# Sandwich block on one core: loading and splitting the weights in place, first token tile chunk by chunk, its gate and up products first

## The chip, the cores and the metric

The kernel runs on 1 core of one Trainium2 chip. The metric is the device time of one launch in microseconds (us). All arrays are float32. TensorE multiplies in a reduced format (fp32r), so the kernel splits each operand into a high part (rounded) and a low part (the rest), and three matmuls stand for one exact product: high by low, low by high, high by high.

## The reference, cut to what matters

```python
x = x + _layernorm(_L0_attn_ref(_layernorm(x), w_gate, w_up, w_down))
x = x + _layernorm(_L0_ffn_ref(_layernorm(x), W_gate, W_up, W_down))

def _L0_attn_ref(x, w_gate, w_up, w_down):
    s = jax.nn.silu(jnp.einsum('bsh,ih->bsi', x, w_gate))
    k = int(0.5 * I)
    _, idx = jax.lax.top_k(-jnp.abs(s), k)      # the k smallest |s| of each token
    s = s with those entries set to 0
    s = s * jnp.einsum('bsh,ih->bsi', x, w_up)
    return jnp.einsum('bsi,hi->bsh', s, w_down)
def _L0_ffn_ref(x, W_gate, W_up, W_down):
    return (silu(x @ W_gate.T) * (x @ W_up.T)) @ W_down.T
```

x has 4 x 512 = 2048 tokens of H = 512, and I = 1376. In the first layer half of the 1376 gate values of every token, the smallest in magnitude, are set to zero, so a threshold has to be found for each token.

## The kernel before, in words

The 2048 tokens are 16 tiles of 128 (j = 0 to 15). The second layer follows the first and is not touched by the change.

**A tile of layer 1.** x is normalised on VectorE (`x_stats`, GpSimd's power in `x_rstd`, `x_normalise`); for tiles 0 to 2 TensorE transposes it (`transpose_x`), for later tiles VectorE turns 32 x 32 blocks and a DMA moves them (`move_x`). ScalarE writes the high part (`split_x_hi`), VectorE the low part (`split_x_lo`). TensorE makes 3 gate products and 3 up products (n = 0 to 2, columns of 460, 460 and 456; `product(j, m, n)`, m = 0 gate, m = 1 up), each of 4 chunks of the contraction times 3 matmuls. In `product` a chunk is low weights, low x, high by high, and so on to the next chunk. ScalarE takes the silu of each gate product, VectorE the absolute values and their sum (`abs_values`).

**The search for the threshold.** It is a loop over three engines: ScalarE counts the values below the threshold (`count(j, n)`, n = 0 to 5), GpSimd moves the threshold (`newton(j, n)`, a `move` and a `thr` instruction), ScalarE counts again. Then VectorE reads the exact value off (`find_below`, `find_top`, `find_flag`), zeroes the small ones and multiplies (`select`), and turns blocks (`swap_h`). Four DMAs (`move_h`) bring it to transposed place, ScalarE and VectorE split it (`split_h_hi`, `split_h_lo`), and TensorE multiplies by w_down (`down(j)`, 33 matmuls). y is normalised (`y_stats`, `y_rstd`, `normalise_y`) and added to x. `times_up(j, n)` multiplies by the up product and frees its bank.

**The weights.** w_gate and w_up come in 12 pieces (w = 0 to 11: two chunks of the contraction by the columns of one n, 460 KB), w_down in 6 more (w = 12 to 17, 512 KB). SyncE loads each piece into one of 4 slots of a buffer `stage`; from the fifth on it waits until the slot's last piece has been split (L488). ScalarE copies stage to the high part (L905), VectorE subtracts it from stage and writes the low part (L1234).

**The order.** Every engine's instructions stand in an order written by hand; nothing is planned by costs. Before the change TensorE does gate 0.0, gate 0.1, the transposes of tile 1, gate 0.2, gate 1.0 to 1.2, then up 0.0, up 1.0, up 0.1, up 0.2, transposes of tile 2, up 1.1, up 1.2, then tiles 2 and 3 (from tile 2 on all gate, then all up), with `down(0)` behind gate 3.0 and `down(1)` behind up 3.2. From tile 4 on a loop is used; there `down(j-2)` stands behind up j.2 for j = 4, up j.1 for j = 5, and up j.0 from j = 6 on. VectorE's order begins at L1523, ScalarE's at L1057, SyncE's at L570, GpSimd's at L1806. `keep_busy` are transposes without a use that fill TensorE's first microseconds.

Of the kernel before, what the change touches and what calls it, by code (L numbers as in the profile page):

```python
# [16 lines left out]
def sandwich(nc, x, x_first, w_gate, w_up, w_down, W_gate, W_up, W_down, out):  # L17
# [47 lines left out]
    NSLOT = 4  # L65
# [11 lines left out]
    USEQ = [(0, 0), (1, 0), (0, 1), (0, 2), (1, 1), (1, 2)] + [(j, n) for j in range(2, TILES) for n in range(3)]  # L77
# [68 lines left out]
    with ctx:  # L146
# [22 lines left out]

        with nc.sbuf_tensor("stage", [P, NSLOT, 2, H], F32) as stage:  # L170
            pass
# [72 lines left out]

        prod_flat = prod[:, :, :].rearrange("p a b -> p (a b)")
        SW = KC * GW // 2
        stage_flat = stage[:, :, :, :].rearrange("p s c t -> p (s c t)")
# [101 lines left out]
        stage_in = [sem(f"stage_in{i}") for i in range(NSLOT)]  # L349
# [21 lines left out]
        x_moved = [sem(f"x_moved{i}") for i in range(2)]  # L371
        exact = sem("exact")
# [16 lines left out]
        ring = [("G", 0, 0), ("G", 0, 1), ("G", 0, 2), ("G", 1, 0), ("G", 1, 1), ("G", 1, 2)]  # L389
        ring += [("U", j, n) for j, n in USEQ[:6]]  # L390
        for j in range(2, TILES):
# [38 lines left out]
        def x_bank(a):  # L430

            return (tr_ps[1], tr_ps[2], tr_ps[1])[a]

# [8 lines left out]
        def _(sp):  # L442
# [41 lines left out]
            def load_w(w):  # L484
                m, n, c = PIECES[w]
                slot = w % NSLOT
                if w >= NSLOT:
                    sp.wait_ge(wlo_done, w - NSLOT + 1)  # L488
                if m < 2:
                    src = (w_gate, w_up)[m].rearrange("p (c i) -> p c i", c=KC)[:, c:c + 2, CO[n]:CO[n] + CW[n]]  # L490
                    sp.dma_start(stage[:, slot, :, 0:CW[n]], src).then_inc(stage_in[slot], 16)
                else:
                    src = w_down[n * P:(n + c) * P, :].rearrange("(c q) h -> q c h", q=P)
                    sp.dma_start(stage[:, slot, 0:c, :], src).then_inc(stage_in[slot], 16)
# [90 lines left out]
            for w in range(12, NP - 1):  # L585
# [4 lines left out]
            load_w(NP - 1)  # L590
# [101 lines left out]
        def _(pe):  # L692
# [23 lines left out]

            def product(j, m, n):
# [6 lines left out]
                for c in range(KC):  # L724
                    if j == 0 and c % 2 == 0:
                        pe.wait_ge(wlo_done, 6 * m + 2 * n + c // 2 + 1)
# [130 lines left out]
            product(1, 1, 1)  # L857
            product(1, 1, 2)
# [36 lines left out]
        def _(act):  # L895
            def split_weights_hi(w):
                m, n, c = PIECES[w]
                slot = w % NSLOT
                act.wait_ge(stage_in[slot], 16 * (w // NSLOT + 1))
                if m < 2:  # L900
                    src = stage[:, slot, :, 0:CW[n]]
                    dst = gu_hi[m][:, :].rearrange("p (c i) -> p c i", c=KC)[:, c:c + 2, CO[n]:CO[n] + CW[n]]
                else:
                    src, dst = stage[:, slot, 0:c, :], down_hi[:, n:n + c, :]
                nc.scalar.activation(dst, src, ACT.Copy).then_inc(whi_done, 1)  # L905
# [37 lines left out]
            def split_x_hi(a):  # L943
# [9 lines left out]
                nc.scalar.activation(hi, src, ACT.Copy).then_inc(xhi_done, 1)  # L953

# [103 lines left out]
            split_x_hi(0)  # L1058
            for w in range(1, 4):
                split_weights_hi(w)  # L1060
            silu(0, 0)
            split_weights_hi(4)
            split_weights_hi(5)
            silu(0, 1)
            split_x_hi(1)
            split_weights_hi(6)
            silu(0, 2)
            split_weights_hi(7)
            split_weights_hi(8)
# [12 lines left out]
            count(0, 4)
            split_x_hi(2)
            count(0, 5)
            split_weights_hi(13)
            guess(1)
            count(1, 0)
            split_weights_hi(14)
            count(1, 1)
            split_weights_hi(15)  # L1090
            count(1, 2)
            split_weights_hi(16)
            count(1, 3)
            split_x_hi(3)
            count(1, 4)
            silu(2, 0)
            split_h_hi(0)
# [5 lines left out]
            for n in range(4):  # L1103
                count(2, n)
            normalise_y(0)
            count(2, 4)
            split_h_hi(1)
            for j in range(3, TILES - 1):
# [8 lines left out]
                if j < TWO[0]:  # L1117
# [93 lines left out]
        def _(dve):  # L1211
# [11 lines left out]
            def split_weights_lo(w):  # L1223
                m, n, c = PIECES[w]
                slot = w % NSLOT
                dve.wait_ge(whi_done, w + 1)
                if m < 2:
                    src = stage[:, slot, :, 0:CW[n]]
                    hi, lo = (t[m][:, :].rearrange("p (c i) -> p c i", c=KC)[:, c:c + 2, CO[n]:CO[n] + CW[n]]
                              for t in (gu_hi, gu_lo))  # L1230
                else:
                    src = stage[:, slot, 0:c, :]
                    hi, lo = down_hi[:, n:n + c, :], down_lo[:, n:n + c, :]
                nc.vector.tensor_tensor(lo, src, hi.bitcast(F32), ALU.subtract).then_inc(wlo_done, 1)  # L1234
# [12 lines left out]
            def x_normalise(a):  # L1247
# [4 lines left out]
                if p >= FIRST:  # L1252
                    dve.wait_ge(xn_done, p + 1)
                    nc.vector.transpose(xin[:, p % 2, :], xin[:, p % 2, :]).then_inc(xswap_done, 1)

# [268 lines left out]
            x_normalise(0)  # L1524
            split_weights_lo(0)
            split_x_lo(0)
            for w in range(1, 4):
# [392 lines left out]
```

## Time and profile before

| | us |
|---|---|
| median of 3 runs | 725.38 (725.26 to 725.48) |
| the profiled execution | 725.1 |
| its span | 723.3 |
| TensorE busy in the span | 710.0 |
| VectorE busy | 569.3 |
| ScalarE busy | 380.0 |
| GpSimd busy | 246.5 |

The span runs from the first to the last instruction; 1.8 us of the profiled execution lie around it. The granted clock of TensorE was 0.998 of full speed over the span.

### The profile page before, as it was taken

What the parts mean: (1) busy time and instruction counts of PE and PEld (TensorE: products, weight loads), DVE (VectorE), ACT (ScalarE), POOL (GpSimd) and SP (SyncE); (2) the same over time, 40 slices, a digit from 0 to 9 for tenths busy, and PEclk for the clock granted to TensorE, in tenths of its full rate; (3) what the DMA queues carried; (4) which work ended last, traced back from release to release, by engine and by line L of the source; (5) the groups of instructions that cost most, each with busy time, mean ns of one, the idle gap of its engine ahead of it and who ended that gap; (6) DMA issues with size and microseconds to landing.
All of it is one profiled execution on the core that took longest, in us unless ns stands there. A gap on an engine that the chain in (4) does not pass through costs nothing.

```text
span 723.3 us, 9783 instructions
## 1 busy us (share of the span) xinstructions
PE 710.0 (98%) x3193; PEld 596.5 (82%) x3193; DVE 569.3 (79%) x980; ACT 380.0 (53%) x594; POOL 246.5 (34%) x372
## 2 busy tenths in 40 slices
PE   8999999999999999999999999999999999999996
PEld 7888788888888888888888888878877888877885
DVE  7789788889889888896889489987777898876342
ACT  5886577666666756667563234433344333323231
POOL 0422223332222332223241156613456665621001
PEclk9999999999999999999999999999999999999999
DMA  8641424333455344554322986345752533334441
GB/s 272 202 111 62 97 70 99 63 82 89 108 128 112 85 96 91 129 118 101 106 89 61 226 254 194 102 139 133 210 138 78 156 117 117 100 101 140 143 136 44
DMA packets 126214, 88.56 MB, mean 122 GB/s; under 512 B 66416, under 2 KB 106608, under 8 KB 126160
## 3 DMA queue, kind: packets, MB, share of 16 engines
q1 hardware_dynamic: 126160, 87.91, 45.0%
q8 instruction: 25, 0.41, 0.2%
q14 instruction: 29, 0.24, 0.1%
HBM read 49.87 MB, written 18.87 MB: 95 GB/s over the span
## 4 chain that ended last, share of the span: by engine, by line
PE 71%; DVE 8%; issue 7%; POOL 6%; ACT 5%; DMA 2%; SPq 0%; DVEq 0%; POOLq 0%; ACTq 0%
PE gu_ps L804 13%; PE y_ps L745 13%; PE gu_ps L731 11%; PE tr_ps L804 10%; PE tr_ps L731 8%; PE gu_ps L826 5%; PE tr_ps L826 4%; PE gu_ps L779 3%; PE tr_ps L779 3%; ACT junk L928 2%; POOL move L1769 1%; DMA stage<-in_L_attn_w_gate 1%; POOL yrstd L1753 1%; DVE below L1363 1%; POOL thr L1772 1%
## 5 line engine op out<-in xcount | busy, mean ns | idle before, releaser
L928 ACT ACTIVATE junk<-absv,thr 128x1383 bf16<-128x1383 f32 x96 | 139.1, 1449 | 42.9 <-POOL thr L1772 42.1
L745 PE MATMUL y_ps<-down_hi,hT 128*128 128x512 f32 x352 | 109.0, 391 | 0.0
L1769 POOL TENSOR_SCALAR move<-sgn 128x1 f32<-128x1 f32 x80 | 42.4, 530 | 107.6 <-ACT junk L928 107.5
L745 PEld LDWEIGHTS y_ps<-down_hi,hT 128*128 128x128 f32 x352 | 66.1, 188 | 14.4
L745 PE MATMUL y_ps<-down_lo,hT 128*128 128x512 f32 x176 | 69.3, 394 | 0.4 <-DVE hT L1273 0.4
L731 PE MATMUL gu_ps<-gate_hi,xT 128*128 128x460 f32 (+1 forms) x232 | 67.5, 372 | 0.0
L731 PE MATMUL gu_ps<-up_hi,xT 128*128 128x460 f32 (+1 forms) x232 | 67.2, 371 | 0.0
L1753 POOL TENSOR_TENSOR yrstd<-yvar,half 128x1 f32<-128x1 f32 x32 | 22.3, 696 | 91.8 <-DVE yvar L1282 91.7
L731 PEld LDWEIGHTS gu_ps<-gate_hi,xT 128*128 128x128 f32 x232 | 43.9, 189 | 4.9
L731 PEld LDWEIGHTS gu_ps<-up_hi,xT 128*128 128x128 f32 x232 | 43.6, 188 | 5.1
L1746 POOL TENSOR_TENSOR xrstd<-xvar,half 128x1 f32<-128x1 f32 x32 | 22.9, 715 | 68.6 <-DVE xvar L1245 68.5
L1804 POOL TENSOR_TENSOR prod<-prod,gate_lo_raw 128x512 f32<-128x512 f32 (+1 forms) x18 | 23.9, 1327 | 64.7 <-DVE prod L1492 64.7
L731 PE MATMUL gu_ps<-gate_lo,xT 128*128 128x460 f32 (+1 forms) x116 | 43.7, 377 | 1.6 <-DVE xT L1267 1.5
L731 PE MATMUL tr_ps<-gate_hi,xT 128*128 128x460 f32 (+1 forms) x152 | 44.1, 371 | 0.0
L731 PE MATMUL tr_ps<-up_hi,xT 128*128 128x460 f32 (+1 forms) x152 | 44.0, 371 | 0.0
L731 PE MATMUL gu_ps<-up_lo,xT 128*128 128x460 f32 (+1 forms) x116 | 43.2, 373 | 0.0
L1762 POOL TENSOR_SCALAR unit<-gains,asum 128x5 f32<-128x5 f32 x16 | 9.0, 562 | 99.8 <-DVE absv L1312 99.7
L745 PEld LDWEIGHTS y_ps<-down_lo,hT 128*128 128x128 f32 x176 | 33.1, 188 | 7.9 <-issue 1.1
L1403 DVE SCALAR_TENSOR_TENSOR prod<-absv,kth,prod 128x1376 f32<-128x1376 f32 x16 | 26.4, 1653 | 14.5 <-DVE anyflag L1394 9.6
L1029 ACT ACTIVATE gate_hi_raw<-gate_hi_raw 128x512 f32<-128x512 f32 (+1 forms) x18 | 11.4, 632 | 50.1 <-DVE gate_hi_raw L1456 50.1
L826 PE MATMUL gu_ps<-down_hi,h_two 128*128 128x512 f32 x120 | 37.3, 392 | 0.0
L1772 POOL TENSOR_SCALAR thr<-move,step,thr 128x1 f32<-128x1 f32 x80 | 33.0, 413 | 9.0
(312 smaller groups left out, 1890.2 us busy)
## 6 DMA issues: line engine op xcount, KB each, us to landing
absv<-prod SPq DMA_DIRECT2D x64, 176.0 KB, 3.4
h_scratch<-prod SPq DMA_DIRECT2D x38, 256.0 KB, 2.8
xin<-x_scratch SPq DMA_DIRECT2D x18, 256.0 KB, 3.0
xres<-in_L_attn_x SPq DMA_DIRECT2D x16, 256.0 KB, 3.6
x_scratch<-xres SPq DMA_DIRECT2D x16, 256.0 KB, 2.8
xg_even<-xin SPq DMA_DIRECT2D x64, 64.0 KB, 2.5
up_lo<-h_scratch SPq DMA_DIRECT2D x8, 512.0 KB, 3.7
up_hi<-h_scratch SPq DMA_DIRECT2D x8, 512.0 KB, 4.3
```

The lines of the kernel that those rows point to most:

```text
L731: last = nc.tensor.matmul(dst[:, 0:CW[n]], xt, w, start=(c == 0 and i == 0), stop=(c == KC - 1 and i == 2))
L745: last = nc.tensor.matmul(y_ps[:, :], h, w[:, c, :], start=(c == 0 and i == 0), stop=(c == JC - 1 and i == 2))
L779: last = nc.tensor.matmul(quad_bank(u, n)[0:k, :], w[:, rows], xt[:, cols], start=(a in (1, 7) and c == 0 and i == 0), stop=(a in (2, 4) a ...
L804: last = nc.tensor.matmul(m_bank(u, i)[0:k, :], w[:, rows], xt[:, cols], start=(c == 0 and n3 == 0), stop=(c == 1 and n3 == 2))
L826: nc.tensor.matmul(y_bank(b)[:, :], h[:, toks], w[:, j, :], start=(j == 0 and i == 0), stop=False)
L928: nc.scalar.activation(junk[:, 0:I + PAD], absv[:, q, A0 - PAD:A0 + I], ACT.Sign, bias=thr[:, q:q + 1], scale=-1.0, accum_out=sgn[:, q:q + ...
L1403: nc.vector.scalar_tensor_tensor(prod[:, q, 0:I], values(q), kth[:, 0:1], prod[:, q, 0:I], ALU.is_gt, ALU.mult).then_inc(h_done, 1)
L1746: nc.gpsimd.tensor_tensor(xrstd[:, :], xvar[:, :], half[:, :], ALU.pow).then_inc(xr_done, 1)
L1753: nc.gpsimd.tensor_tensor(yrstd[:, q:q + 1], yvar[:, q:q + 1], half[:, :], ALU.pow).then_inc(yr_done, 1)
L1769: stepped(nc.gpsimd.tensor_scalar(move[:, :], sgn[:, q:q + 1], sgn[:, q:q + 1], float((WINDOW - 1) ** 2) + 0.5, ALU.mult, ALU.is_gt))
L1772: nc.gpsimd.tensor_scalar(thr[:, q:q + 1], move[:, :], step[:, :], thr[:, q:q + 1], ALU.mult, ALU.add).then_inc(thr_done, 1)
L1804: nc.gpsimd.tensor_tensor(at, at, s_part("gate1", u)[0:width(u), :], ALU.mult).then_inc(h1_done, 1)
```

## The change

The four edits below belong to the first 100 us or so. The loop of tiles 4 to 14 and all of layer 2 stay as they are.

1. A raw piece of weights lands in the place of its own low part instead of in a slot; SyncE's waits for a slot are gone. The three special waits between the first loads go too, and x tile 1 is issued before piece 2.
2. x tile 0 is handled in 4 chunks of 128 columns by all engines: 4 normalising instructions, 4 transposes into 4 different PSUM banks with a semaphore step each, 4 high copies, 4 subtractions.
3. Tile 0's gate and up products come first (12 pieces of weights, tile 0 alone), then tile 1's. Inside one of tile 0's products the 8 matmuls with high weights come first, and the 4 with low weights last.
4. The orders of ScalarE, VectorE, GpSimd and SyncE are rewritten up to tile 3. Among other things x tile 4 is split before tile 3's turn in the loop, and `newton(2, 2)` comes after `y_rstd(0)`.

```diff
+        def raw_w(w):
+            m, n, c = PIECES[w]
+            if m == 2:
+                return down_lo_raw[:, n:n + c, :]
+            raw = (gate_lo_raw, up_lo_raw)[m][:, :].rearrange("p (c i) -> p c i", c=KC)
+            return raw[:, c:c + 2, CO[n]:CO[n] + CW[n]]
...
-                if w >= NSLOT:
-                    sp.wait_ge(wlo_done, w - NSLOT + 1)
+                sp.dma_start(raw_w(w), src).then_inc(piece_in[w], 16)
...
             load_w(0)
             load_w(1)
-            sp.wait_ge(x_in[0], 16)
-            load_w(2)
-            sp.wait_ge(stage_in[0], 16)
-            load_w(3)
-            sp.wait_ge(stage_in[1], 16)
             load_x(1)
-            for w in range(4, 8):
+            for w in range(2, 8):
                 load_w(w)
             load_x(2)
-            for w in range(8, 12):
+            for w in range(8, GU_PIECES):
                 load_w(w)
             load_x(3)
-            for w in range(12, NP - 1):
+            for w in range(GU_PIECES, NP):
                 load_w(w)
...
+            def first_product(m, n):
+                what = ("GU"[m], 0, n)
+                bank_free(what)
+                dst = bank(what)
+                for c in range(KC):
+                    if (m, n) == (0, 0):
+                        if c < KC - 1:
+                            pe.wait_ge(xlo_part, c + 1)
+                        else:
+                            pe.wait_ge(xlo_done, 1)
+                    if c % 2 == 0:
+                        pe.wait_ge(whi_done, 6 * m + 2 * n + c // 2 + 1)
+                    at = c * I + CO[n]
+                    for s in (1, 0):
+                        nc.tensor.matmul(dst[:, 0:CW[n]], xT[:, 0, s, c * P:(c + 1) * P], gu_hi[m][:, at:at + CW[n]],
+                                         start=(c == 0 and s == 1), stop=False)
+                for c in range(KC):
+                    if c % 2 == 0:
+                        pe.wait_ge(wlo_done, 6 * m + 2 * n + c // 2 + 1)
+                    at = c * I + CO[n]
+                    last = nc.tensor.matmul(dst[:, 0:CW[n]], xT[:, 0, 0, c * P:(c + 1) * P], gu_lo[m][:, at:at + CW[n]],
+                                            start=False, stop=(c == KC - 1))
+                last.then_inc((g_done, u_done)[m], 1)
...
             pe.wait_ge(consts, 2)
-            keep_busy(15)
-            transpose_x(0)
-            keep_busy(10)
-            for n in range(2):
-                product(0, 0, n)
+            keep_busy(18)
+            transpose_first_x()
+            keep_busy(4)
+            for n in range(3):
+                first_product(0, n)
+            first_product(1, 0)
+            first_product(1, 1)
             transpose_x(1)
-            product(0, 0, 2)
+            first_product(1, 2)
             for n in range(3):
                 product(1, 0, n)
-            for j, n in USEQ[:4]:
-                product(j, 1, n)
             transpose_x(2)
-            product(1, 1, 1)
-            product(1, 1, 2)
+            for n in range(3):
+                product(1, 1, n)
```

ScalarE's new order up to the loop is: piece 0; x tile 0 in chunks; pieces 1 to 4; silu 0.0; pieces 5, 6; silu 0.1; pieces 7, 8; silu 0.2; pieces 9 to 11; x tile 1; guess 0, count 0.0; piece 12; count 0.1; silu 1.0; count 0.2; silu 1.1; count 0.3; silu 1.2; x tile 2; counts 0.4, 0.5; guess 1, count 1.0; then pieces 13, 14, 15, 16 behind counts 1.0, 1.1, 1.2, 1.3; x tile 3; count 1.4; h tile 0; silu 2.0; piece 17; count 1.5; silu 2.1, 2.2; guess 2, counts 2.0 to 2.2; `normalise_y(0)`; count 2.3; h tile 1; count 2.4; x tile 4.

VectorE's new order is:

```diff
             x_stats(0)
-            x_normalise(0)
-            split_weights_lo(0)
-            split_x_lo(0)
-            for w in range(1, 4):
+            first_x_normalise()
+            for c in range(KC):
+                split_first_x_lo(c)
+            for w in range(7):
                 split_weights_lo(w)
             x_stats(1)
+            split_weights_lo(7)
             x_normalise(1)
...
+            for w in range(8, GU_PIECES):
+                split_weights_lo(w)
             split_x_lo(1)
...
             abs_values(0)
...
             x_stats(2)
+            for n in range(3):
+                times_up(0, n)
             x_normalise(2)
             x_stats(3)
-            split_weights_lo(9)
+            split_weights_lo(12)
             x_normalise(3)
...
             abs_values(1)
...
             split_x_lo(2)
...
             find_below(0)
             find_top(0)
-            times_up(1, 1)
+            for n in range(3):
+                times_up(1, n)
             find_flag(0)
             select(0)
             swap_h(0)
             split_weights_lo(13)
...
             split_weights_lo(14)
             split_x_lo(3)
             split_weights_lo(15)
             split_weights_lo(16)
-            find_below(1)
             split_h_lo(0)
             split_weights_lo(17)
+            find_below(1)
             find_top(1)
             abs_values(2)
-            x_stats(4)
             find_flag(1)
             select(1)
+            swap_h(1)
+            x_stats(4)
+            times_up(2, 0)
             x_normalise(4)
-            swap_h(1)
-            for n in range(3):
-                times_up(2, n)
             y_stats(0)
+            times_up(2, 1)
+            times_up(2, 2)
+            x_stats(5)
             add_residual(0)
             split_h_lo(1)
-            x_stats(5)
             x_normalise(5)
             for j in range(3, TILES - 1):
                 a = XSEQ[POS[j + 1]:]
+                if j == 3:
+                    split_x_lo(j + 1)
                 find_below(j - 1)
```

## Rows read from the trace of the kernel before

**Rows 1.** The page: busy us, share of the span and instructions per engine
```profile
PE 710.0 (98%) x3193; PEld 596.5 (82%) x3193; DVE 569.3 (79%) x980; ACT 380.0 (53%) x594; POOL 246.5 (34%) x372
```

**Rows 2.** Waits of TensorE, whole span: us in total, times, longest us
```profile
PE gu_ps L731 <- DVE xT L1267: 1.5, 1, 1.5
PE y_ps L745 <- DVE hT L1273: 0.4, 2, 0.2
```

**Rows 3.** Chain that ended last, 80 to 240 us: start us, us, what
```profile
100.19 1.65 DVE below L1363
143.24 0.61 DVE hT L1273
143.99 7.80 PE y_ps L745 x33
174.42 5.00 PE tr_ps L731 x24
```

**Rows 4.** Timeline of TensorE's matmuls: start us, us, work [idle before <- releaser]
```profile
8.88 0.73 PE L731 MATMUL gu_ps<-gate_lo,xT 128*128 128x460 f32 x1
25.35 0.37 PE L731 MATMUL gu_ps<-up_lo,xT 128*128 128x460 f32 x1
58.46 0.39 PE L745 MATMUL y_ps<-down_lo,hT 128*128 128x512 f32 x1
87.81 0.45 PE L731 MATMUL gu_ps<-gate_lo,xT 128*128 128x460 f32 x1 [1.51 <-DVE xT L1267]
```

**Rows 5.** Windows: stretch and length, busy of engines, granted clock, DMA share, GB/s
```profile
3.00:6.00 3.00, 2.15 (x11) 1.75 (x10) 1.58 (x4) 0.94 (x1) 0.56 (x1) 1.00 1.03 382
7.00:22.00 15.00, 14.87 (x71) 13.33 (x70) 12.86 (x17) 11.24 (x15) 2.25 (x2) 1.00 0.87 281
426.00:430.00 4.00, 4.00 (x19) 3.24 (x19) 3.78 (x6) 0.45 (x1) 0.82 (x2) 1.00 0.95 367
```

**Rows 6.** Timeline of VectorE, 0 to 90 us
```profile
3.53 0.70 DVE L1241 BATCH_NORM_STATS2 xstat<-xin 128x6 f32<-128x512 f32 x1 [1.93 <-DMA xin<-in_x_first]
...
5.37 0.55 DVE L1250 TENSOR_SCALAR xin<-xin,xmv,xrstd 128x512 f32<-128x512 f32 x1 [0.74 <-POOL xrstd L1746]
...
14.08 2.21 DVE L1234 TENSOR_TENSOR gate_lo<-stage,gate_hi 128x912 fp32r<-128x912 f32 x2
...
18.61 1.59 DVE L1312 SCALAR_TENSOR_TENSOR absv<-prod 128x1376 f32<-128x1376 f32 x1 [0.51 <-ACT prod L940]
...
47.62 1.65 DVE L1258 STREAM_TRANSPOSE prod<-prod 128x1408 f32<-128x1408 f32 x1
...
52.57 2.35 DVE L1234 TENSOR_TENSOR down_lo<-stage,down_hi 128x1024 fp32r<-128x1024 f32 x2
...
69.18 1.60 DVE L1258 STREAM_TRANSPOSE prod<-prod 128x1408 f32<-128x1408 f32 x1
...
82.31 1.61 DVE L1363 SCALAR_TENSOR_TENSOR below<-absv,thr 128x1376 f32<-128x1376 f32 x1
...
85.47 1.57 DVE L1312 SCALAR_TENSOR_TENSOR absv<-prod 128x1376 f32<-128x1376 f32 x1
```

**Rows 7.** Timeline of ScalarE, 40 to 66 us
```profile
40.34 1.45 ACT L928 ACTIVATE junk<-absv,thr 128x1383 bf16<-128x1383 f32 x1
...
43.06 1.44 ACT L928 ACTIVATE junk<-absv,thr 128x1383 bf16<-128x1383 f32 x1
...
55.30 0.56 ACT L940 ACTIVATE prod<-tr_ps 128x460 f32<-128x460 f32 x1 [2.42 <-DMA absv<-prod]
...
62.67 1.45 ACT L928 ACTIVATE junk<-absv,thr 128x1383 bf16<-128x1383 f32 x1
...
65.09 1.45 ACT L928 ACTIVATE junk<-absv,thr 128x1383 bf16<-128x1383 f32 x1 [0.55 <-POOL thr L1772]
```

**Rows 8.** Timeline of GpSimd, 50 to 92 us
```profile
52.64 2.35 POOL L1769 TENSOR_SCALAR move<-sgn 128x1 f32<-128x1 f32 x1 [1.67 <-ACT junk L928]
...
91.37 1.09 POOL L1769 TENSOR_SCALAR move<-sgn 128x1 f32<-128x1 f32 x1 [1.67 <-ACT junk L928]
```

More of the change, by code:

```diff
@@ L76, in sandwich @@
     GSEQ = [(j, n) for j in range(TILES) for n in range(3)]
-    USEQ = [(0, 0), (1, 0), (0, 1), (0, 2), (1, 1), (1, 2)] + [(j, n) for j in range(2, TILES) for n in range(3)]
+    USEQ = GSEQ
     G_AT = {what: k + 1 for k, what in enumerate(GSEQ)}
@@ L168, in sandwich @@
         down_lo = sb("down_lo", [P, JC, H], F32R)
-        with nc.sbuf_tensor("stage", [P, NSLOT, 2, H], F32) as stage:
+        with nc.sbuf_tensor("stage", [P, KC * 2 * GW], F32) as stage_flat:
             pass
@@ L347, in res_buf @@
             return xin[:, b % 2, :] if in_xin(b) else xres[:, b % 2, :]
-        stage_in = [sem(f"stage_in{i}") for i in range(NSLOT)]
+        piece_in = [sem(f"piece_in{w}") for w in range(NP)]
         pair_in = [sem(f"pair_in{i}") for i in range(NPAIR)]
@@ L385, in sandwich @@
         block = ctx.enter_context(nc.Block())
-        ring = [("G", 0, 0), ("G", 0, 1), ("G", 0, 2), ("G", 1, 0), ("G", 1, 1), ("G", 1, 2)]
-        ring += [("U", j, n) for j, n in USEQ[:6]]
-        for j in range(2, TILES):
+        ring = []
+        for j in range(TILES):
             ring += [("G", j, n) for n in range(3)] + [("U", j, n) for n in range(3)]
@@ L589, in _ @@
             move_h(0)
-            load_w(NP - 1)
             load_res(0)
@@ L953, in split_x_hi, with split_first_x_hi @@
                 nc.scalar.activation(hi, src, ACT.Copy).then_inc(xhi_done, 1)
+            def split_first_x_hi():
+                hi, _ = x_place(0)
+                for c in range(KC):
+                    if c < KC - 1:
+                        act.wait_ge(x_tr_part, c + 1)
+                    else:
+                        act.wait_ge(x_tr, 1)
+                    nc.scalar.activation(hi[:, c, :], first_x_bank(c),
+                                         ACT.Copy).then_inc(xhi_part if c < KC - 1 else xhi_done, 1)
             def split_h_hi(j):
@@ L1102, in _ @@
             guess(2)
-            for n in range(4):
+            for n in range(3):
                 count(2, n)
             normalise_y(0)
+            count(2, 3)
+            split_h_hi(1)
             count(2, 4)
-            split_h_hi(1)
+            split_x_hi(4)
             for j in range(3, TILES - 1):
@@ L1558, in _ @@
             split_weights_lo(13)
-            times_up(1, 2)
             split_weights_lo(14)
@@ L1808, in _ @@
             units(0)
+            newton(0, 0)
             x_rstd(2)
-            newton(0, 0)
+            newton(0, 1)
             x_rstd(3)
-            for n in range(1, STEPS):
+            for n in range(2, STEPS):
                 newton(0, n)
@@ L1817, in _ @@
             units(2)
+            newton(2, 0)
+            newton(2, 1)
             x_rstd(4)
-            for n in range(4):
-                newton(2, n)
             y_rstd(0)
+            newton(2, 2)
+            x_rstd(5)
+            newton(2, 3)
             newton(2, 4)
-            x_rstd(5)
             for j in range(3, TILES - 1):
```

101 lines of the change are left out of this document (51 added, 50 removed).

## The prediction, made before the changed kernel had run

> **What bounds the kernel now.** First the busy shares on the page: TensorE is busy 710.0 us of 723.3 [rows 1], so the change can win no more than TensorE's idle time, some 13 us in all. Then TensorE's waits: in the stretch that the change touches there is one of 1.5 us, before gate 4.0, for the low part of x tile 4, and two of 0.2 us before `down(3)` and `down(4)` for the low part of h [rows 2]. Third the chain that ended last: from 143.99 us on it is TensorE without a break, and before that it runs over VectorE, ScalarE and GpSimd, the search for the threshold, up to the low part of h tile 4 at 143.24 [rows 3]. So two things race to `down(4)` at 143.99: TensorE's stream, and the search. They arrive within 0.2 us of each other. Whatever moves the later of them at that point moves the end; a gain in one alone is worth 0.2 us there. The reader should then see in TensorE's timeline the points that I follow: first product at 8.88, seventh product at 25.35, `down(0)` at 58.46, gate 4.0 at 87.81 [rows 4]. A product is 5.00 / 2 = 2.50 us, a `down` 7.6 us [rows 3].
>
> **Edit 1, the loads.** Before, up to 4 pieces are under way and the DMA engines moved 281 GB/s from 7 to 22 us; with more queued they moved 382 GB/s (3 to 6 us) and 367 (426 to 430 us) [rows 5]. x tile 0 is there at 3.53 [rows 6]; from then to piece 11 there are 12 pieces and x tiles 1 and 2, 6.16 MB. At 380 GB/s piece 11 lands at 3.53 + 16.2 = 19.7, at 281 GB/s at 25.4. I take 380, as the queue is now never empty; both ends are kept. The first pieces keep their place if the queue is served in order, which the landing of x tile 0 ahead of the pieces issued right behind it suggests.
>
> The Trainium skill puts the limit of memory for one core at about 358 GB/s (DMA: Bandwidth & Descriptors, Specifications). By it piece 11 would land at 20.7, an estimate, 1.0 later than by the row, and the sum below would grow by 0.3. The rows go both ways: 382 in the one, 367 in the other.
>
> **Edit 2, chunks.** Statistics start at 3.53 and normalising at 5.37 as before. A quarter of a normalisation, transpose, copy and subtraction each follow one another; the whole ones ended with the low part at 8.44 (VectorE also did piece 0 in between). A quarter of 0.55 us is 0.15 to 0.25, so I put the low part's end at 7.45 (bounds 6.9 and 8.4) and TensorE's first product at 7.4 instead of 8.88. This 1.5 us is lost again at once, since tile 0 alone needs all 12 pieces. Three more instructions on ScalarE, VectorE and the queue each cost nothing beyond that; the different number of `keep_busy` is covered by the wait for x.
>
> **Edit 3, tile 0 first.** Who is last now? VectorE. Two low parts of weights take 2.21 us overlapped, 1.07 each [rows 6], 12 take 12.8. Among them stand tile 1's statistics (1.1: the 1.84 between the two starts less 0.74 of idle time [rows 6]) and its normalisation, 0.55, for which VectorE will wait some 0.6, because GpSimd's power is issued while piece 7 is being subtracted (see below). 7.45 + 12.8 + 1.1 + 0.6 + 0.55 = 22.5; low part of x tile 1 0.65: 23.1; `abs_values(0)` 23.1 to 24.7, where it was 18.61. ScalarE has piece 11 high by 20.7, ahead of it. TensorE: up 0.1 ends with piece 9 at 20.8, transposes 0.6, up 0.2 2.5: its seventh product starts at 24.0 instead of 25.35, 1.35 us earlier, with gaps in between that are worth nothing. So TensorE gains 1.35 and the search starts 4.5 us later.
>
> **How GpSimd stands to VectorE.** A `move` of 1 column takes 0.3 us as a rule; the one at 52.64 took 2.35, while VectorE subtracted pieces 15 and 16 from 52.57 to 54.92, and the one at 91.37 took 1.09, during a `select` that ended at 92.31 [rows 6, 8]. So a step of GpSimd waits until VectorE has done with such two-input instructions, through several if they are back to back.
>
> **Edit 4, the search of tiles 0 to 3.** A count with its step to the next is 2.42 us, with a piece of w_down in between 2.72 [rows 7].
> Tile 0: first count at 24.9. With 1.0 us of collisions (piece 12's low part) and the silus in between, count 0.5 ends at 40.3 and count 1.0 starts at 40.5, where it was 40.34 [rows 7]: the interleaved splits have gone from it, and that pays for the late start. VectorE: `find_below(0)` 38.7, top, three `times_up` of 0.55 (one before), flags and `select` 3.3, `swap_h(0)` ends at 50.0 instead of 49.27. h is in place 6.0 after that (49.27 to 55.30 [rows 6, 7]): 56.0.
> Tile 1: counts at 43.2, 46.0, 49.1 (0.4 lost to `select(0)`). `newton(1, 3)` is due at 50.7. Then VectorE has pieces 13 and 14, x tile 3, pieces 15 and 16 almost back to back from 50.0 to 55.4, so that the threshold comes at 55.7. Before, a `times_up` between pieces 13 and 14 left the gap. What is queued behind count 1.4 on ScalarE (55.8 to 57.6) is h tile 0: its high part starts at 57.6, the low part's first group ends at 58.9, and `down(0)` starts there, 0.4 later than at 58.46 [rows 4] though TensorE is free at 57.1. Then `find_below(1)`, now behind h and piece 17, about 60.8, `swap_h(1)` ends at 71.9 (69.18 + 1.60 = 70.78 before [rows 6]), h tile 1 at 77.9.
> Tile 2: `newton(2, 2)` is now behind `y_rstd(0)`, which waits for `y_stats(0)`, now behind x tile 4 on VectorE. That ends at about 75.8, count 2.3 starts at 77.6. Behind it on ScalarE stand h tile 1 (79.3), count 2.4 (80.8) and x tile 4 (82.6). `down(1)` can start at 80.5; TensorE was free at 58.9 + 7.6 + 12.5 = 79.0. Gate 4.0 then starts at 88.1 instead of 87.81: the wait of 1.5 us is gone, and 1.5 us of wait stands before `down(1)` and 1.75 before `down(0)`.
> Tile 3: `find_below(2)` starts at 83.9 instead of 82.31, `abs_values(3)` at 87.0 instead of 85.47 [rows 6], 1.5 later. One thing is given back: the low part of x tile 4 no longer stands between `abs_values(3)` and the flags, so `select(2)` is 0.6 earlier against the counts and the collision of 91.37 is shorter by that. Search: + 0.9 from `find_below(3)` (100.19 [rows 3]) on, to `down(4)` at 144.9.
> TensorE alone, 0.3 late at gate 4.0 and with both waits of 0.2 us to use up [rows 2], would be there at 143.99 + 0.3 - 0.4 = 143.9. The later wins: + 0.95 us.
>
> **The other edits** (waits of SyncE, other semaphores, a different ring of PSUM banks) I cost at nothing. The tightest bank is that of up 3.2, freed by `times_up(2, 1)` at 76.4, when TensorE gets there; if it is late, the 1.5 us of wait before `down(1)` cover it. The price without that cover would be up to 1 us.
>
> **The sum.** 725.1 (the profiled execution: span 723.3 and 1.8 around it) + 0.95 = 726.05; the median of the runs is 0.28 above the profiled execution, so 726.3.
>
> **Rivals.**
> A. The search is not held up at tile 1: VectorE leaves GpSimd a gap between piece 14 and x tile 3, or the power at piece 7 isn't blocked. For it: VectorE has to wait 0.2 us for x tile 3 there. Against it: a `move` and a `thr` need 0.7. Everything from h tile 0 on moves up 1.5 to 2.2 us: search - 0.6 to - 1.2, about 724.4.
> B. The search has slack that I don't see and TensorE's stream alone decides: 1.35 early, the 1.51 wait and both of 0.2 us gone, 725.38 - 3.2 = 722.2. For it: on TensorE these are all the gaps. Against it: the search was on the chain all the way to 143.24.
> C, on the other side. The loads are no faster than before. At 281 GB/s piece 11 lands at 25.4 and its low part ends at 27.4, against 22.5: the search starts 4.9 us later than I count and all of this arrives, 731.2; at 320 GB/s it lands at 22.8, the low part ends at 24.9, 2.4 later, 728.7. It decides from a rate under some 360. For it: 281 over 15 us with the engines 0.87 busy. Against it: two stretches with a full queue. That the loads all at once delay pieces 0 and 1 belongs here.
> D. More collisions of GpSimd with VectorE than I count, each 0.5 to 2 us, above all `thr` of tile 0 behind piece 12: 727.5.
>
> **How the numbers follow.** My forecast, 725.4 to 727.0, 0.42; A 0.2; B 0.1; C 0.13; D 0.15. This kernel's runs tell 0.2% (1.45 us) from no change, so "within" is 723.9 to 726.8. Of my forecast nearly all lies within, of A three quarters, of D a quarter, of C little; that gives faster 0.22, within 0.48, slower 0.30. The range of 723.2 to 728.6 leaves out B's best and C's worst.
>
> **What the profile after would show.** Right: over 350 GB/s from 4 to 19 us; the seventh product near 24.0; `abs_values(0)` near 23; a `move` of about 4 us on GpSimd at 50.7 to 55; waits of TensorE before `down(0)` and `down(1)` of over 1 us and none before gate 4.0; `normalise_y(0)` between counts 2.2 and 2.3 with ScalarE idle before it; `down(4)` near 144.9. Wrong: `down(1)` without a wait, `abs_values(3)` before 85.5, or piece 11 after 21.

## The result and the profile after

| | before | after |
|---|---|---|
| median of 19 runs, us | 725.26 (724.51 to 726.2) | 726.06 (725.15 to 727.47) |
| profiled execution, us | 725.1 | 726.0 |
| its span, us | 723.3 | 724.2 |
| ratio to before, 95% interval | | 1.0015 (1.0008 to 1.0022) |

The change makes the kernel 0.80 us slower, 0.11% by the medians and 0.15% by the ratio. That is inside the 0.2% that I called "within"; with 19 runs on each side it can still be told from nothing. The forecast was + 0.95 us, a median of 726.3.

TensorE's waits from 0 to 100 us, after (us in total, times, longest us). Before, the same stretch has the one of 1.5 us [rows 2] and two in the first microseconds, of 1.7 and 0.9; the second and third line here are those two:

```profile
PE y_ps L778 <- DVE hT L1328: 2.8, 2, 1.4
PE y_ps L875 <- DVE prod L1262: 1.7, 1, 1.7
PE tr_ps L724 <- DVE xin L1299: 0.6, 1, 0.6
PE tr_ps L748 <- DVE up_lo L1273: 0.3, 1, 0.3
PE gu_ps L748 <- DVE up_lo L1273: 0.2, 1, 0.2
```

TensorE's timeline after: start us, us, work, in brackets the idle time before it and its releaser. The answers to [rows 4] are the seventh product, `down(0)`, and in place of gate 4.0, which has no wait now, `down(1)`:

```profile
24.22 0.37 PE L764 MATMUL gu_ps<-gate_lo,xT 128*128 128x460 f32 x1
...
58.87 0.47 PE L778 MATMUL y_ps<-down_lo,hT 128*128 128x512 f32 x1 [1.39 <-DVE hT L1328]
80.59 0.47 PE L778 MATMUL y_ps<-down_lo,hT 128*128 128x512 f32 x1 [1.37 <-DVE hT L1328]
```

The wait of 1.51 us has gone, and 1.39 and 1.37 us have come before `down(0)` and `down(1)`. The seventh product is 1.13 earlier than at 25.35, `down(0)` 0.41 later than at 58.46.

The chain that ended last, after (start us, us, what), against [rows 3]:

```profile
100.90 1.65 DVE below L1418
...
144.12 0.61 DVE hT L1328
144.74 0.14 issue
144.87 7.81 PE y_ps L778 x33
```

`find_below(3)` is 0.71 later and `down(4)` 0.88 later than at 143.99; the span is 0.9 longer. From there on nothing has moved, the whole difference is made before 144 us. The chain at that point is the search; that the search makes the difference is what the experiments test.

VectorE's timeline after, against [rows 6], and two windows of the loads (length, busy of five engines, granted clock, DMA share, GB/s), against [rows 5]:

```profile
7.54 5.68 DVE L1273 TENSOR_TENSOR gate_lo<-gate_lo_raw,gate_hi 128x920 fp32r<-128x920 f32 x5
...
23.27 1.58 DVE L1367 SCALAR_TENSOR_TENSOR absv<-prod 128x1376 f32<-128x1376 f32 x1
...
53.18 2.35 DVE L1273 TENSOR_TENSOR down_lo<-down_lo_raw,down_hi 128x1024 fp32r<-128x1024 f32 x2
...
86.78 1.57 DVE L1367 SCALAR_TENSOR_TENSOR absv<-prod 128x1376 f32<-128x1376 f32 x1
```

```profile
4.00:19.00 15.00, 14.13 (x69) 11.42 (x68) 13.28 (x24) 11.64 (x17) 1.92 (x2) 1.00 1.03 379
```

```profile
6.00:19.00 13.00, 12.75 (x60) 10.28 (x61) 12.09 (x20) 10.67 (x16) 1.36 (x1) 1.00 1.04 388
```

The loads run at 379 GB/s (4 to 19 us), where the kernel before had 281 from 7 to 22 us, and the search of tile 0 still starts 4.66 us later than at 18.61, since it stands behind all 12 pieces. `abs_values(3)` (86.78 against 85.47) is 1.31 late, but that is not a rest of the 4.66. `find_below(0)` and count 1.4 show it, first before, then after:

```profile
38.84 1.64 DVE L1363 SCALAR_TENSOR_TENSOR below<-absv,thr 128x1376 f32<-128x1376 f32 x1
51.01 1.45 ACT L928 ACTIVATE junk<-absv,thr 128x1383 bf16<-128x1383 f32 x1 [0.15 <-POOL thr L1772]
```

```profile
38.72 1.68 DVE L1418 SCALAR_TENSOR_TENSOR below<-absv,thr 128x1376 f32<-128x1376 f32 x1 [0.55 <-POOL thr L1823]
55.62 1.45 ACT L959 ACTIVATE junk<-absv,thr 128x1383 bf16<-128x1383 f32 x1 [3.08 <-POOL thr L1823]
```

At `find_below(0)` the late start has been made up in full. The lag is made anew at tile 1, where count 1.4 waits 3.08 us for GpSimd's `thr` and comes 4.61 late.

### The profile page after: what moved, and what is told of

Its sections match the earlier page's. It is cut to its first block, busy times and chain, and to the rows that moved or that the text cites. A ratio compares the mean times of both kernels' runs of the same rounds, so it can differ in the third digit from the quotient of the medians.

```text
span 724.2 us, 9786 instructions
## 1 busy us (share of the span) xinstructions
PE 709.0 (98%) x3190; PEld 594.0 (82%) x3190; DVE 570.6 (79%) x986; ACT 380.9 (53%) x597; POOL 247.6 (34%) x372
## 4 chain that ended last, share of the span: by engine, by line
PE 71%; DVE 9%; issue 6%; ACT 6%; POOL 5%; DMA 2%; SPq 1%; DVEq 0%; POOLq 0%; ACTq 0%
PE gu_ps L837 13%; PE y_ps L778 13%; PE gu_ps L764 11%; PE tr_ps L837 10%; PE tr_ps L764 8%; PE gu_ps L859 5%; PE tr_ps L859 4%; PE gu_ps L812 3%; PE tr_ps L812 3%; ACT junk L959 2%; POOL yrstd L1804 1%; POOL thr L1823 1%; POOL move L1820 1%; DMA gate_lo_raw<-in_L_attn_w_gate 1%; PE y_ps L859 1%
## 5 line engine op out<-in xcount | busy, mean ns | idle before, releaser
L1820 POOL TENSOR_SCALAR move<-sgn 128x1 f32<-128x1 f32 x80 | 40.0, 500 | 106.4 <-ACT junk L959 106.4
L764 PE MATMUL gu_ps<-gate_hi,xT 128*128 128x460 f32 (+1 forms) x216 | 62.6, 371 | 0.0
L764 PE MATMUL gu_ps<-up_hi,xT 128*128 128x460 f32 (+1 forms) x208 | 60.3, 371 | 0.0
L1855 POOL TENSOR_TENSOR prod<-prod,gate_lo_raw 128x512 f32<-128x512 f32 (+1 forms) x18 | 23.5, 1304 | 65.4 <-DVE prod L1547 65.4
L764 PEld LDWEIGHTS gu_ps<-gate_hi,xT 128*128 128x128 f32 x216 | 40.6, 188 | 4.7
L764 PEld LDWEIGHTS gu_ps<-up_hi,xT 128*128 128x128 f32 x208 | 39.1, 188 | 4.6
L764 PE MATMUL tr_ps<-gate_hi,xT 128*128 128x460 f32 (+1 forms) x144 | 41.7, 371 | 0.0
L764 PE MATMUL gu_ps<-gate_lo,xT 128*128 128x460 f32 (+1 forms) x108 | 40.2, 372 | 0.0
L1823 POOL TENSOR_SCALAR thr<-move,step,thr 128x1 f32<-128x1 f32 x80 | 36.5, 456 | 9.1
L764 PE MATMUL gu_ps<-up_lo,xT 128*128 128x460 f32 (+1 forms) x104 | 38.7, 372 | 0.0
L1328 DVE TENSOR_TENSOR hT<-absv,hT 128x512 fp32r<-128x512 f32 (+1 forms) x48 | 28.1, 641 | 12.0 <-ACT hT L1002 11.9
```

The lines of the kernel that those rows point to most:

```text
L764: last = nc.tensor.matmul(dst[:, 0:CW[n]], xt, w, start=(c == 0 and i == 0), stop=(c == KC - 1 and i == 2))
L1328: nc.vector.tensor_tensor(lo, raw, hi.bitcast(F32), ALU.subtract).then_inc(hlo_done, 1)
L1820: stepped(nc.gpsimd.tensor_scalar(move[:, :], sgn[:, q:q + 1], sgn[:, q:q + 1], float((WINDOW - 1) ** 2) + 0.5, ALU.mult, ALU.is_gt))
L1823: nc.gpsimd.tensor_scalar(thr[:, q:q + 1], move[:, :], step[:, :], thr[:, q:q + 1], ALU.mult, ALU.add).then_inc(thr_done, 1)
L1855: nc.gpsimd.tensor_tensor(at, at, s_part("gate1", u)[0:width(u), :], ALU.mult).then_inc(h1_done, 1)
```

## The experiments

Each ratio compares the runs with those of the kernel before in the same session. The kernel before had medians of 725.26 with the changed kernel, 725.28 with e1 to e4, 725.50 with e5 to e7, 725.48 with e8 to e10 and 725.64 with e11 and e12, so medians of different sessions can differ by 0.4 us for no reason of the kernel. Where two kernels with an edit are compared below, the difference of their ratios is given with an interval that I estimate from the two. "Late start" is used for a profiled execution in which the first pieces came late (`abs_values(0)` is its mark), since single executions differ by up to 1.2 us there.

| kernel | median, us | ratio to before (95%) | abs_values(0) | down(4) |
|---|---|---|---|---|
| changed | 726.06 | 1.0015 (1.0008, 1.0022) | 23.27 | 144.87 |
| e1_gap | 725.57 | 1.0005 (0.9996, 1.0014) | 23.42 | 143.75 |
| e2_tile2 | 725.92 | 1.0004 (0.9995, 1.0013) | 23.52 | 144.38 |
| e3_both | 725.00 | 0.9997 (0.9988, 1.0006) | 24.50 | 143.94 |
| e4_busy | 726.53 | 1.0016 (1.0007, 1.0025) | 24.27 | 145.67 |
| e5_slots | 729.49 | 1.0052 (1.0039, 1.0066) | 25.68 | 147.21 |
| e6_whole | 726.65 | 1.0018 (1.0009, 1.0027) | 24.08 | 145.67 |
| e7_inplace | 725.07 | 0.9993 (0.9984, 1.0002) | 18.70 | 143.60 |
| e8_first | 726.23 | 1.0009 (1.0000, 1.0018) | 23.36 | 145.17 |
| e9_w12 | 724.51 | 0.9992 (0.9983, 1.0001) | 23.00 | 143.31 |
| e10_all | 724.78 | 0.9989 (0.9980, 0.9998) | 23.06 | 143.27 |
| e11_x4 | 725.70 | 0.9999 (0.9990, 1.0008) | 18.18 | 143.76 |
| e12_w12 | 724.30 | 0.9980 (0.9971, 0.9989) | 24.09 | 143.04 |

### Letting GpSimd through at tile 1

```diff
             split_x_lo(3)
+            dve.wait_ge(thr_done, STEPS + 4)
             split_weights_lo(15)
```

> The changed kernel with one wait more: VectorE holds piece 15's low part until newton(1, 3) is through. Theory (S): the search for the threshold sets the time up to down(4), and at tile 1 it is held by GpSimd's thr of 2.92 us at 52.67, behind x tile 3 and pieces 15 and 16. The added wait lets thr through at about 53.6, count 1.4 starts at 53.7 instead of 55.62, h tile 0 is split when its DMA has landed (56.25 instead of 57.39), down(0) starts at 57.7 instead of 58.87, and down(4) at 143.8 instead of 144.87: 1.1 us faster than the changed kernel, 725.0. Rival (P): TensorE's own stream or another wait sets it, and waits only change places: no change, 726.1.

GpSimd in the changed kernel, then in e1_gap:

```profile
50.83 1.73 POOL L1820 TENSOR_SCALAR move<-sgn 128x1 f32<-128x1 f32 x1 [1.67 <-ACT junk L959]
52.67 2.92 POOL L1823 TENSOR_SCALAR thr<-move,step,thr 128x1 f32<-128x1 f32 x1
```

```profile
50.98 1.73 POOL L1821 TENSOR_SCALAR move<-sgn 128x1 f32<-128x1 f32 x1 [1.67 <-ACT junk L959]
52.82 0.82 POOL L1824 TENSOR_SCALAR thr<-move,step,thr 128x1 f32<-128x1 f32 x1
```

One wait more on VectorE, which had 2.50 us without work there, takes 2.1 us from the `thr`. `down(0)` starts at 57.58 without a wait, `down(4)` at 143.75, 1.12 earlier, as expected. In the ratio 0.7 us arrive against the changed kernel, with about 0.8 us on each side, so the times alone don't show it. In the trace the search sets `down(4)`; rival P falls.

### Tile 2: the step of the search before y's statistics

```diff
             x_rstd(4)
-            y_rstd(0)
             newton(2, 2)
+            y_rstd(0)
-            x_rstd(5)
             newton(2, 3)
+            x_rstd(5)
...
-            normalise_y(0)
-            count(2, 3)
+            count(2, 3)
+            normalise_y(0)
             split_h_hi(1)
```

> The changed kernel with newton(2, 2) before y_rstd(0) again, normalise_y(0) behind count 2.3 and h tile 1 behind it. Theory (S): ScalarE's 4.14 us of idle time before normalise_y(0) is on the search; count 2.3 then starts at 74.1 instead of 77.33, h tile 1's high part at 77.9 instead of 79.11, down(1) at 79.3 instead of 80.59, down(4) at 143.7: 1.2 us faster than the changed kernel, 724.9. Rival (P): no change, since pieces of the search behind it wait for VectorE or for the DMA of h anyway.

ScalarE's waits in the changed kernel, 0 to 100 us (us in total, times, longest us), then its timeline in e2_tile2:

```profile
ACT y_ps L1008 <- POOL ybias L1806: 4.1, 1, 4.1
```

```profile
76.90 0.75 ACT L1008 ACTIVATE y_ps<-y_ps,ybias,yrstd 128x512 f32<-128x512 f32 x1 [0.67 <-POOL ybias L1805]
78.76 1.56 ACT L1002 ACTIVATE hT<-absv 128x512 fp32r<-128x512 f32 x3 [1.10 <-DMA absv<-prod]
```

The 4.1 us go down to 0.7, and h tile 1 is then late: its DMAs land at 78.76, 6.8 us after `swap_h(1)` ends at 71.91, not 6.0. So `down(1)` starts at 80.26 instead of 79.3, and `down(4)` is 0.5 earlier, with a start 0.25 later, not 1.2. Theory S is right in kind, and half of its gain or more is taken by the next wait, the landing of h, as its rival P said; the times alone (725.92, the ratio 1.0004) don't decide.

### Both together

> Both edits of the two kernels beside it together. Theory (S): the gains add, as one is at tile 1 and the other at tile 2: 2.3 us faster than the changed kernel, 723.8, and 1.4 faster than the kernel before; down(4) at 142.6. Rival (P): TensorE's stream takes over after the first of them, 725.0 or later.

The median is 725.00 against 726.06, and by the ratios e3_both is 1.3 us faster than the changed kernel, with 0.8 on each side: the gain is clear of noise. The profiled execution has a late start of 1.23 us, and `down(4)` is 0.93 earlier all the same. Against the same start that is 2.16 if a start is passed on in full, and then the gains add up; e9_w12 below shows that it isn't always, so 2.16 is an upper bound. The median is 1.2 above the 723.8 that I expected: e3_both is level with the kernel before.

### Work for TensorE in its wait

```diff
             product(3, 0, 0)
+            keep_busy(5)
             down(0)
```

> The changed kernel with 5 more transposes without a use on TensorE (about 1.1 us) right before down(0), where it waits 1.39 us. Theory (S): the wait hides them, down(0) stays at 58.9 and the time at 726.1. Rival (P): TensorE's stream sets the time and 1.1 us come on top, 727.2.

TensorE's timeline in e4_busy:

```profile
58.34 0.71 PE L875 MATMUL y_ps<-ident 128*128 128x128 f32 x5
59.87 0.47 PE L778 MATMUL y_ps<-down_lo,hT 128*128 128x512 f32 x1 [0.82 <-DVE hT L1329]
```

The transposes took only 0.71 us here, and lie in the wait. `down(0)` is 1.00 later with a start 1.00 later, and `down(4)` 0.80 later, so they cost nothing. The ratio, 1.0016, is the changed kernel's 1.0015.

### The loads throttled, pieces 4 to 11

```diff
             def load_w(w):
                 m, n, c = PIECES[w]
+                if 4 <= w < GU_PIECES:
+                    sp.wait_ge(wlo_done, w - 3)
```

> The changed kernel, pieces still in place, but from piece 4 to 11 SyncE waits for the low part of the piece four before, as with the slots. Theory (L): tile 0 first needs the full queue. Piece 11 is then issued when piece 7's low part is done, 17.7, and lands near 22.5 instead of 20.2; abs_values(0) comes 2 to 3 us later than 23.27, and the whole search with it: 728.5. Rival: VectorE sets the pace of the start alone, under 0.5 us later, 726.5.

`abs_values(0)` is 2.41 later and `down(4)` 2.34 later, so up to there what the start loses goes through. The profiled execution is longer by more, 3.6 us of span: behind `down(4)` another 1.2 are lost, 0.62 of them in a wait of TensorE before 452.31, in layer 2, that the changed kernel doesn't have; why it comes up stays open. The median is 3.43 above the changed kernel's; by the ratios, which leave the sessions out, it is 2.7 with 1.1 on each side. Tile 0 first can only be had with the full queue, as rival C of the prediction has it.

### x tile 0 whole again

```diff
-            transpose_first_x()
+            transpose_x(0)
...
-            first_x_normalise()
-            for c in range(KC):
-                split_first_x_lo(c)
+            x_normalise(0)
+            split_x_lo(0)
```

> The changed kernel with x tile 0 normalised, transposed and split whole again. Theory: VectorE is busy from there on to abs_values(0), so its first piece's low part, 0.9 us later than 7.54, moves abs_values(0) and the search by as much: 0.9 slower than the changed kernel, 727.0. Rival (as in my prediction's working): the chunks earn nothing, since tile 0 has to wait for its weights anyway: 726.1.

VectorE in e6_whole gets to the weights at 8.10, not 7.54:

```profile
7.49 0.69 DVE L1320 TENSOR_TENSOR xT<-tr_ps,xT 128x512 fp32r<-128x512 f32 x1 [1.38 <-ACT xT L982]
8.10 2.13 DVE L1271 TENSOR_TENSOR gate_lo<-gate_lo_raw,gate_hi 128x920 fp32r<-128x920 f32 x2
```

`abs_values(0)` and `down(4)` are both 0.8 later, and it looks as if the chunks had earned most of it. But VectorE isn't busy without a break from there to `abs_values(0)`, as my theory had it: it waits 0.26 us for ScalarE's copy of piece 2, and that copy waits for the piece to land.

```profile
10.49 3.52 DVE L1271 TENSOR_TENSOR gate_lo<-gate_lo_raw,gate_hi 128x920 fp32r<-128x920 f32 x3 [0.26 <-ACT gate_hi L934]
```

ScalarE's copy of piece 2 in the changed kernel, in e6_whole and in e12_w12 (a kernel further down, which has the chunks), then `abs_values(0)` in e6_whole and in e12_w12:

```profile
8.69 0.97 ACT L936 ACTIVATE gate_hi<-gate_lo_raw 128x920 fp32r<-128x920 f32 x1 [0.53 <-DMA gate_lo_raw<-in_L_attn_w_gate]
```

```profile
9.49 0.97 ACT L934 ACTIVATE gate_hi<-gate_lo_raw 128x920 fp32r<-128x920 f32 x1 [0.88 <-DMA gate_lo_raw<-in_L_attn_w_gate]
```

```profile
9.51 0.97 ACT L936 ACTIVATE gate_hi<-gate_lo_raw 128x920 fp32r<-128x920 f32 x1 [0.89 <-DMA gate_lo_raw<-in_L_attn_w_gate]
```

```profile
24.08 1.58 DVE L1365 SCALAR_TENSOR_TENSOR absv<-prod 128x1376 f32<-128x1376 f32 x1
```

```profile
24.09 1.58 DVE L1366 SCALAR_TENSOR_TENSOR absv<-prod 128x1376 f32<-128x1376 f32 x1
```

Piece 2 came 0.80 later here, and that is all of the 0.8. With the chunks and piece 2 equally late, e12_w12 starts its search at the same time. In the profiles of the changed kernel, e1 to e4, e6, e9 and e12 `abs_values(0)` follows this copy by 14.58 to 14.70 us, with the chunks or without. The ratios, 1.0018 and 1.0015, overlap too. So no run shows that the chunks earn anything, and the rows speak for the rival. In an execution with an early start they could be worth up to 0.37 us, an estimate: the 0.56 less the 0.19 that VectorE waits for ScalarE at 13.40 in the changed kernel.

### Edit 1 alone

The kernel before with pieces landing in place, one semaphore each, and without the slots' and the early waits of SyncE.

> The kernel before with edit 1 alone: raw pieces in the place of their low part, no waits for slots, the early waits of SyncE gone. Theory: the old order needed little of it. TensorE's 0.37 us in front of gate 0.2 goes, abs_values(0) comes 0.4 earlier than 18.61, and the search follows by 0 to 0.5: 724.9 to 725.3. Rival: the slots held the old order back too, and the loads' full rate gives 1 us or more: 724.3.

The median is 725.07 against 725.50 in that session, the interval holds 1. `abs_values(0)` did not move (18.70), so the expected way was wrong: instead `find_below(0)` is 0.92 earlier (37.92), because the `move` of 1.41 us that GpSimd had at 30.71 before is no longer held by VectorE (0.40 at 30.80), which is 0.9 ahead by then, as it no longer waits for x tile 2. `down(4)` is 0.39 earlier.

### The first loads protected

```diff
             load_w(1)
-            load_x(1)
-            for w in range(2, 8):
+            sp.wait_ge(x_in[0], 16)
+            load_w(2)
+            load_w(3)
+            load_x(1)
+            for w in range(4, 8):
```

> The changed kernel, but piece 2 and all behind it are issued only when x tile 0 has landed, and x tile 1 behind piece 3, as in the kernel before. In the profiled executions of e3_both, e4_busy and e6_whole the DMA engines moved only 246 to 256 GB/s from 4 to 6 us and ScalarE got piece 1 at 7.6 to 8.1 instead of 7.2; abs_values(0) came 0.8 to 1.2 late. Theory (Q): pieces behind in the full queue take part of the rate from piece 1 in some executions; with the wait piece 1 is there by 7.0 in all, abs_values(0) at 23.0 to 23.4, the times spread less (within 1 us) and the median is 0.5 lower than the changed kernel's, 725.6. Rival: the late piece 1 is chance of the memory, whatever is queued: same median and spread, 726.1, or the wait leaves the queue empty and piece 2 comes late, 726.6.

DMA windows from 4 to 6 us, in e3_both and in e8_first:

```profile
4.00:6.00 2.00, 1.94 (x10) 1.54 (x8) 1.19 (x6) 0.97 (x1) 0.56 (x1) 1.00 0.94 246
```

```profile
4.00:6.00 2.00, 2.00 (x11) 1.67 (x9) 1.19 (x7) 0.97 (x1) 0.56 (x1) 1.00 0.97 319
```

The median isn't lower. The changed kernel itself had 318 GB/s in its profiled execution, so the pair above shows a late and an early start and not what the wait does. The 11 runs lie within 1.26 us, where the 19 of the changed kernel span 2.3; but e10_all, with the same wait, spans 1.95, and e12_w12, without it, 1.45. Of the eight profiles with a full queue and without this wait (the changed kernel, e1 to e4, e6, e9, e12) four have a late start (e3, e4, e6, e12), and of the two with it (e8, e10) neither. That is too few to say that the full queue delays the first pieces; the cause stays open.

What the wait costs can be seen, and it is what the rival expected in kind, a queue that runs short, though not at piece 2. ScalarE waits for piece 4 instead:

```profile
11.18 0.97 ACT L939 ACTIVATE gate_hi<-gate_lo_raw 128x912 fp32r<-128x912 f32 x1 [0.91 <-DMA gate_lo_raw<-in_L_attn_w_gate]
```

In the changed kernel it is at 11.11 there. Piece 12 is late as well: ScalarE waits 0.47 us for it at 27.55, where the changed kernel doesn't wait, and count 0.1 starts at 28.52, not at 27.86. In e10_all these waits are 0.88 and 0.50.

### Piece 12 out of the way

```diff
             x_stats(3)
-            split_weights_lo(12)
             x_normalise(3)
+            split_weights_lo(12)
```

> e3_both, and piece 12's low part behind x_normalise(3), where VectorE has 2.9 us without work. Theory (S with GpSimd held by VectorE): the thr of 1.29 us at 31.11 goes down to 0.34, every count from 0.2 on is 0.95 earlier, and the search still sets the time: down(4) at about 142.9 with a late start as in e3_both, at 141.8 with an early one; 0.9 faster than e3_both, 724.1. Rival (P): TensorE's stream takes over, under 0.3 faster, 724.8.

GpSimd in e9_w12:

```profile
29.61 0.34 POOL L1823 TENSOR_SCALAR thr<-move,step,thr 128x1 f32<-128x1 f32 x1
29.91 0.57 POOL L1797 TENSOR_TENSOR xrstd<-xvar,half 128x1 f32<-128x1 f32 x1
31.62 1.38 POOL L1820 TENSOR_SCALAR move<-sgn 128x1 f32<-128x1 f32 x1 [1.15 <-ACT junk L959]
```

A miss: the `thr` is free, and the next `move` runs into piece 12 instead (VectorE from 31.73 to 32.91). `find_below(0)` comes 15.58 after `abs_values(0)`, where it was 15.45. The median is 0.5 below that of e3_both, and the ratios don't tell the two apart.

`down(4)` is a miss too: 143.31 with an early start, where I expected 141.8. `abs_values(0)` is 1.50 earlier than in e3_both and `down(4)` only 0.63. Part of the lead is lost where h lands: ScalarE waits 0.86 us for h tile 0 and 1.13 for h tile 1 (0.51 and 0.88 in e3_both), and their copies start 1.02 and 0.77 earlier than there. An earlier start is not passed on in full.

> e9_w12 with the order of the first loads of e8_first: the sum of all four. Theory: the gains add up, 0.5 from the first loads on 0.9 from piece 12: 723.6, faster than the kernel before by 1.7. Rival (P): TensorE's stream, which can't be at down(4) before 141.1 plus its late start, or the h DMAs set the time, 724.3 to 724.8.

e10_all adds the first loads of e8_first to it and is level with e9_w12 (724.78 and 724.51); its gain of 0.5 did not come either, and the late piece 12 of e8_first is there again.

### Piece 12 after the next step

```diff
             x_normalise(3)
+            dve.wait_ge(thr_done, 3)
             split_weights_lo(12)
```

> e9_w12, with one wait more: piece 12's low part only when newton(0, 2) is through. In e9_w12 piece 12 left the thr of newton(0, 1) alone (0.34 instead of 1.29 us), but met the move of newton(0, 2) at 31.62, which then took 1.38. Theory (S with GpSimd held by VectorE): now neither is held, find_below(0) comes 15.6 after abs_values(0) minus 1.0, so 14.6, near 37.7; the search gains 1.0 less what select(0) or the DMAs take back, down(4) near 142.5, 723.7. Rival: another collision or the landing of h takes it all, 724.5.

GpSimd in e12_w12:

```profile
32.72 0.30 POOL L1821 TENSOR_SCALAR move<-sgn 128x1 f32<-128x1 f32 x1 [1.15 <-ACT junk L959]
33.13 0.34 POOL L1824 TENSOR_SCALAR thr<-move,step,thr 128x1 f32<-128x1 f32 x1
```

Now `find_below(0)` follows `abs_values(0)` by 14.52, as expected, and with a start 0.82 late `down(4)` is at 143.04, 1.83 earlier than in the changed kernel (I had 142.5). The median of 724.30 is the lowest of all, though 0.6 above the 723.7 that I expected. It is 1.3 under the kernel before in that session, ratio 0.9980 (0.9971 to 0.9989), and by the ratios 2.5 us under the changed kernel, with 0.8 on each side: with three small edits to the order the new kernel beats both. How much of this the last one brings is not shown by the times; its ratio and that of e9_w12 overlap.

### x tile 4 early, alone

The kernel before, with `split_x_hi(4)` behind `split_h_hi(1)` and `split_x_lo(4)` ahead of `find_below(2)`.

> The kernel before, with x tile 4 split early as in the change (high part behind h tile 1 on ScalarE, low part ahead of find_below(2) on VectorE) and nothing else. Theory (S): the wait of 1.51 us before gate 4.0 goes, but the search is no earlier, find_below(2) even 0.7 later, of which 0.6 comes back at select(2); TensorE waits before down(2) to down(4) instead, down(4) stays within 0.3 of 143.99 and the time at 725.4. Rival (P), the rival B of the prediction: TensorE's stream has the say, 1.5 us faster, 723.9.

```profile
102.31 0.47 PE L745 MATMUL y_ps<-down_lo,hT 128*128 128x512 f32 x1 [1.25 <-DVE hT L1274]
123.17 0.47 PE L745 MATMUL y_ps<-down_lo,hT 128*128 128x512 f32 x1 [0.49 <-DVE hT L1274]
143.76 0.48 PE L745 MATMUL y_ps<-down_lo,hT 128*128 128x512 f32 x1 [0.29 <-DVE hT L1274]
```

TensorE's timeline shows what became of the 1.51 us: 1.25 of it now stands before `down(2)`, `down(4)` is 0.23 earlier, with a start 0.43 earlier, and the time is the same. The one wait of TensorE in this stretch was worth nothing by itself. Rival B of the prediction, 1.5 us or more for it, falls.

## Why the prediction was right

- **What bounds it.** The race of TensorE and the search up to `down(4)`. e4_busy and e11_x4 show that at the waits before `down(0)` and gate 4.0 TensorE's side costs nothing. e1_gap shows in the trace, and e3_both and e12_w12 in the times as well, that less time in the search is a shorter kernel.
- **Edit 1.** 380 GB/s taken, 379 measured from 4 to 19 us. ScalarE waits for piece 11 until 20.16, where I had it landing at 19.7; 6.16 MB from 3.53 on make 370 GB/s, as the rate is lower in the first microseconds. By the Trainium skill's limit of about 358 GB/s (DMA: Bandwidth & Descriptors, Specifications) it would have been there at 20.7. The rate over 13 us was 388 GB/s, above that figure, so the measurement decides against it as a limit for this case, where one core runs.
- **Edit 2.** VectorE starts on the pieces at 7.54 (7.45 in the sum). That term has hardly any weight: the rows of e6_whole and e12_w12 show piece 2 deciding when the search starts.
- **Edit 3.** `abs_values(0)` 23.27 (23.1), seventh product 24.22 (24.0). The sum takes VectorE as the last from the first piece on. In the trace that holds from piece 6 on; before, it waits for ScalarE and the landing, 0.2 us in all here and up to 1.4 with a late start. The sum has no term for late pieces; rival C alone speaks of it. Of the eight profiles named at e8_first four start at 23.0 to 23.5 and four at 24.1 to 24.5.
- **Edit 4.** `down(0)` 58.87 (58.9), `down(1)` 80.59 (80.5), `abs_values(3)` 86.78 (87.0), `down(4)` 144.87 (144.9). The last is closer than the working behind it: `find_below(3)` is 0.71 late, not 0.9, and a late start, as in e4_busy and e6_whole, puts `down(4)` at 145.67. So the mechanism is right, and the agreement to 0.03 us is luck. The waits before `down(0)` and `down(1)` are 1.39 and 1.37 (1.75 and 1.5). GpSimd behind VectorE was the largest single term: I had put it in one `move` of 4 us; it was a `move` of 1.73 and a `thr` of 2.92.
- **The rivals.** A (a gap for GpSimd) did not happen, but e1_gap made it: 1.1 us, where I had 1.5 to 2.2. C was averted by the full queue, and e5_slots measures what it would have cost at 315 GB/s from 6 to 19 us: 2.7 us by the ratios (C had 2.4 at 320). D did not happen: the collision at piece 12 was there with the 1.0 us counted. The time rose by 0.80 us, 0.15 less than the sum; the median, 726.06, is 0.24 below its 726.3.

## What to carry to other kernels

Where TensorE's stream and a chain over the small engines meet, look for the point up to which the chain that ended last leaves TensorE; a wait of TensorE before that point may be worth nothing, and a microsecond in the chain up to one: 2.34 of 2.41 came through in e5_slots, but 0.63 of 1.50 between e3_both and e9_w12. When an order is rewritten, go through the chain's GpSimd steps and see what VectorE does at each: a block of long two-input subtractions put back to back there costs GpSimd the whole block, and a wait that holds VectorE back for 0.25 us (e1_gap) or 0.60 (e12_w12) can make the chain faster. Moving the block isn't enough if the next step runs into it. And before a late start is put down to an edit, look whether the loads came as early in both traces: in e6_whole they hadn't, and that was the whole difference.

## What the runs showed of the hardware

- A GpSimd instruction on 1 column, 0.3 us by itself, took 2.92 us behind three VectorE subtractions in a row, and 0.82 once the last two were held back. That VectorE's two-input instructions and GpSimd contend is in the Trainium skill too (GPSIMD Engine Reference, Specifications); that a waiting one isn't let in between two back to back is what these rows show.
- With the loads queued and no waits between them the DMA engines moved 388 GB/s for 13 us into this one core.
- From 4 to 6 us, in the same order of loads, they moved 318 GB/s in one execution (the changed kernel), 246 in another (e3_both) and 216 in a third (e12_w12), and the start of the search came 1.2 and 0.8 us later in the latter two. The runs of the changed kernel spread over 2.3 us, those before over 1.7.
